# A decoder layer's self-attention: one bank of the first maxima copied aside by ScalarE, and the context products moved from POOL to VectorE

## What is computed

```python
x = x + _L0_attn_ref(_layernorm(x, axis=-1), Wq, Wk, Wv, Wo, rel_bias)

# _L0_attn_ref: H, DK = 16, 64
q, k, v = (proj(Wq), proj(Wk), proj(Wv))
scores = jnp.einsum('bhqd,bhkd->bhqk', q, k)
bias = rel_bias[_relative_position_buckets(S)]
scores = scores + bias.transpose(2, 0, 1)[None]
attn = jax.nn.softmax(scores, axis=-1)
ctx = jnp.einsum('bhqk,bhkd->bhqd', attn, v)
return ctx.transpose(0, 2, 1, 3).reshape(B, S, H * DK) @ Wo.T
```

## Time and profile before

| | us |
|---|---|
| median of three runs (lowest, highest) | 3798.07 (3797.63, 3800.9) |
| the profiled execution's own time | 3797.64 |
| its span, first to last instruction | 3795.8 |
| mean granted TensorE clock | 0.989 |

### The profile page before, as it was taken

How to read it: one execution, slowest core, us unless ns; L and a number is a source line. 1 busy time by engine, 2 the same in 40 slices (tenths; PEclk the granted TensorE clock), 3 DMA queues, 4 the chain that set the end, 5 groups by cost and what they waited for, 6 DMA issues and landing times. The chain is left out here.

```text
span 3795.8 us, 62609 instructions
## 1 busy us (share of the span) xinstructions
PE 3681.4 (97%) x21277; PEld 2195.6 (58%) x21277; DVE 2450.3 (65%) x3356; ACT 2016.1 (53%) x3452; POOL 2684.2 (71%) x1402
## 2 busy tenths in 40 slices
PE   9989999999999999999999999999979999997899
PEld 7755545555555555554555555555438888884387
DVE  3456676666666766776667776677526777774731
ACT  3336566666666665666666665666534555553232
POOL 1119999999999999999999999999963434430010
PEclk9989999999999999999999999999989999998999
DMA  7662223432234352243223333233322333335710
GB/s 222 160 145 64 70 70 82 103 76 69 70 74 106 100 139 70 70 106 83 72 68 71 99 89 72 67 72 89 92 79 76 104 97 106 105 125 197 248 37 23
DMA packets 368346, 366.60 MB, mean 97 GB/s; under 512 B 189339, under 2 KB 261531, under 8 KB 362776
## 3 DMA queue, kind: packets, MB, share of 16 engines
q1 hardware_dynamic: 299064, 336.50, 32.9%
q10 hardware_dynamic: 67168, 20.98, 2.4%
q0 software_dynamic: 1920, 6.29, 0.5%
HBM read 142.64 MB, written 89.70 MB: 61 GB/s over the span
## 5 line engine op out<-in xcount | busy, mean ns | idle before, releaser
L354 POOL TENSOR_TENSOR acc<-acc,probs 128x1024 f32<-128x1024 f32 x894 | 2131.8, 2385 | 147.0 <-ACT probs L822 35.5
L947 DVE TENSOR_REDUCE maxes<-ps 128x2 f32<-128x1024 f32 x1024 | 1251.3, 1223 | 474.2 <-PE ps L617 462.2
L825 ACT ACTIVATE probs<-ps,far_bias 128x1024 f32<-128x1024 f32 (+7 forms) x1280 | 999.0, 819 | 722.2 <-DVE near_s L964 447.1
L648 PE MATMUL ps<-probs,v_head 128*64 128x512 f32 x4096 | 993.7, 606 | 0.4 <-ACT probs L822 0.4
L636 PE MATMUL ps<-stacks 64*128 64x512 f32 x6144 | 810.9, 392 | 6.1 <-ACT probs L822 5.3
L636 PEld LDWEIGHTS ps<-stacks 64*128 64x128 f32 x6144 | 579.9, 186 | 133.3 <-ACT probs L822 12.6
L617 PE MATMUL ps<-stacks 64*128 64x512 f32 x2048 | 504.1, 490 | 17.5 <-DVE maxes L947 12.2
L617 PEld LDWEIGHTS ps<-stacks 64*128 64x128 f32 x2048 | 191.5, 184 | 565.1 <-DVE maxes L947 424.2
L648 PEld LDWEIGHTS ps<-probs,v_head 128*64 128x64 f32 x4096 | 248.6, 136 | 443.2 <-issue 441.8
L964 DVE TENSOR_TENSOR near_s<-ps,near_bias 128x384 f32<-128x384 f32 (+2 forms) x576 | 265.0, 491 | 37.2 <-PE ps L636 34.3
L970 DVE TENSOR_TENSOR c_q<-ps,c_q 64x512 fp32r<-64x512 f32 x128 | 87.5, 684 | 306.6 <-ACT c_q L781 306.6
(11 more groups left out here) (278 smaller groups left out, 4557.6 us busy)
## 6 DMA issues: line engine op xcount, KB each, us to landing
stacks<-c_q SPq DMA_DIRECT2D x128, 256.0 KB, 4.3
stacks<-c_d SPq DMA_DIRECT2D x64, 512.0 KB, 6.9
stacks<-c_k SPq DMA_DIRECT2D x32, 768.0 KB, 5.6
stacks<-c_k SPq DMA_DIRECT2D x64, 384.0 KB, 7.2
scr_v<-probs ACTq DMA_DIRECT2D x32, 512.0 KB, 4.1
v_head<-scr_v SPq DMA_DIRECT2D x32, 512.0 KB, 3.7
scr_ctx<-ctx_out SPq DMA_DIRECT2D x128, 128.0 KB, 2.3
both_ctx<-scr_ctx SPq DMA_DIRECT2D x32, 512.0 KB, 3.9
```

The lines of the kernel that those rows point to most:

```text
L354: pool.tensor_tensor(acc[:, qb, :], acc[:, qb, :], pr, ALU.add).then_inc(s["summed"], 1)
L648: mm = pe.matmul(ps[64 * half:64 * half + 64, PV, :], v_head[:, side, kt, :], probs[:, st % PT_RING, half * 512:(half + 1) * 512], start=k ...
L825: ins = act.activation(probs[:, st % PT_RING, a:z], sc[:, a:z], ACT.Exp, bias=bias)
L947: dve.tensor_reduce(maxes[:, qt:qt + HALF_GROUPS // 2 + 1:HALF_GROUPS // 2, first_chunk + pair], ps[:, bank:bank + 2, :], AX.X, ALU.max).t ...
```

## The change

ScalarE copies the second of the two banks of the first maxima into a new buffer `aside` (`set_aside`, at the start of each group that has maxima). VectorE's reduction of the first maxima covers the first bank alone, and a further reduction (`largest_aside`), behind that of the second maxima, covers `aside`. TensorE's second maxima wait for the reduction and for the copy; the copy waits for the products and for the reduction of the copy before. The context products go from POOL to VectorE, into groups 14 (`qb` = 0) and 6 (`qb` = 1 of the head before), ahead of the lowering of the queries. In the diff POOL's part comes first, then TensorE's, ScalarE's and VectorE's.

```diff
-CONTEXT_STEPS = {25: 0, 13: 1}
+CONTEXT_GROUPS = {14: 0, 6: 1}
...
+        aside = sb("aside", [P, 512])
...
-            def context(n, qb):
-
-                pool.wait_ge(s["recip_in"], 64 * n + 32 * qb + 32)
-                pool.wait_ge(s["ctx_raw"], 2 * n + qb + 1)
-                pool.tensor_tensor(ctx_out[:], ctx_out[:], sums[:], ALU.mult).then_inc(s["ctx"], 1)
...
-                    if st in CONTEXT_STEPS:
-                        of = CONTEXT_STEPS[st]
-                        if of == 0 or carry:
-                            context(n if of == 0 else n - 1, of)
...
+                if pair == 0:
+                    past(pe, s["aside"], GROUPS * m + turn)
+                elif not (isinstance(n, int) and n < 0):
+                    past(pe, s["aside"], GROUPS * m + turn + 1)
...
+            def set_aside(n, g):
+
+                late, turn = max_turn(g)
+                m = n + 1 if late else n
+                act.wait_ge(s["maxed"], GROUPS * 2 * m + 2 * turn + 1)
+                past(act, s["aside_done"], GROUPS * m + turn)
+                act.copy(aside[:], ps[:, max_bank(n, 0) + 1, :]).then_inc(s["aside"], 1)
...
                 for g in range(GROUPS):
+                    if has_max(n, g):
+                        set_aside(n, g)
                     if g == 0 and prep:
                         split_w(n + 2)
...
-                dve.tensor_reduce(maxes[:, qt:qt + HALF_GROUPS // 2 + 1:HALF_GROUPS // 2, first_chunk + pair], ps[:, bank:bank + 2, :], AX.X, ALU.max).then_inc(s["max_done"], 1)
+                if pair == 0:
+                    dve.tensor_reduce(maxes[:, qt:qt + 1, first_chunk], ps[:, bank, :].unsqueeze(1), AX.X, ALU.max).then_inc(s["max_done"], 1)
+                else:
+                    dve.tensor_reduce(maxes[:, qt:qt + HALF_GROUPS // 2 + 1:HALF_GROUPS // 2, first_chunk + 1], ps[:, bank:bank + 2, :], AX.X, ALU.max).then_inc(s["max_done"], 1)
+
+            def largest_aside(n, g):
+
+                late, turn = max_turn(g)
+                m = n + 1 if late else n
+                qt, first_chunk = max_tiles(turn)
+                dve.wait_ge(s["aside"], GROUPS * m + turn + 1)
+                dve.tensor_reduce(maxes[:, qt + HALF_GROUPS // 2:qt + HALF_GROUPS // 2 + 1, first_chunk], aside[:].unsqueeze(1), AX.X, ALU.max).then_inc(s["aside_done"], 1)
...
                 dve.wait_ge(s["max_done"], GROUPS * 2 * m + GROUPS * (half + 1))
+                dve.wait_ge(s["aside_done"], GROUPS * m + HALF_GROUPS * (half + 1))
...
+            def context(n, qb):
+
+                dve.wait_ge(s["recip_in"], 64 * n + 32 * qb + 32)
+                dve.wait_ge(s["ctx_raw"], 2 * n + qb + 1)
+                dve.tensor_tensor(ctx_out[:], ctx_out[:], sums[:], ALU.mult).then_inc(s["ctx"], 1)
...
                         largest(n, side, g, 1)
+                        largest_aside(n, g)
                     if prep and g in STEP_GROUPS:
                         step(n + 2, STEP_GROUPS[g])
                     if lowered:
                         step_lo(*lowered)
+                    if g in CONTEXT_GROUPS:
+                        qb = CONTEXT_GROUPS[g]
+                        if own if qb == 0 else carry:
+                            context(n if qb == 0 else n - 1, qb)
                     if prep and g in EVAC_GROUPS:
                         queries_low(n + 2, EVAC_GROUPS[g])
```

More of the change, by code:

```diff
@@ L253, in attention @@
             proj q_hi k_own k_hi q_lo step step_hi step_lo fill_q fill_k fill_d
-            maxed max_done neg_ready neg_stored neg_in
+            maxed max_done aside aside_done neg_ready neg_stored neg_in
             scored biased exped summed pved summ sum_out spread recip recip_stored recip_in
```

## The result

The change takes 3844.24 us (median of four runs, 3841.49 to 3847.43) beside 3797.85 for the kernel before on the same chip: a ratio of 1.0120, 95% interval 1.0107 to 1.0132. It is **slower** by 46 us, where 54 us of gain were forecast. The profiled execution took 3841.49, its span is 3839.7, and its mean granted clock 0.980 instead of 0.989. In what follows one execution, of the kernel with the context products alone, took 7044.12 us and is left out of its ratio.

The account below looks back on a forecast made before the run. TensorE (97% busy), losing 0.21 us a group to VectorE's reductions, was taken as the bound, POOL close below. 31 heads x 1.87 = 58, about 2 more, less 6: 54 us off 3798 gives 3744, range 3732 to 3758.

Parts of the forecast that it names:

- TensorE's loop: Second maxima's weight loads wait for VectorE's reduction; halving it to 512 columns gains 0.21 us a group, 1.87 us a head.
- the 1.61 of the sign: Sign of a right forecast: first to second maxima take 1.61 us in most groups instead of 1.82.
- Groups 4 and 12: Groups where ScalarE's copy follows VectorE's step and ScalarE's rounding; second maxima wait, losing 0.23 and 0.14 us.
- the rival of the full gain: Chain behind VectorE's step is not late, since VectorE and ScalarE overlap more: 91 us less 6, 3713 us; chance 0.10.
- The copies on ScalarE cost nothing elsewhere: 16 copies of 0.59, 9.4 us a head, ahead of exponentials that wait for later scores; ScalarE busy 53%; priced at nothing.
- Permission from POOL: Context products off POOL cut its work from 78.7 to 76.2 us a head; otherwise it would limit the gain to 0.8.
- the rival of a bound POOL: Each context product on VectorE keeps POOL from additions some 1.2 us: 78.6 a head, 3776 us; chance 0.13.
- Products on VectorE, covered: In groups 6 and 14 products wait for POOL's addition, up to 2.4 us, then take 0.54; VectorE's idle 2.37 covers them.
- the rival that was slower: Context product misses its turn between POOL's additions and waits another 2.5 us: 3826 to 3900, taken as 3850; chance 0.10.
- The reciprocals' arrival: VectorE waits in order for the reciprocals' broadcast, late in head 13 where SP reloads the input first: +6 us, once.
- the term of 2: 2 us added for the head behind head 13, on top of some 4 us that VectorE is held past its cover.

## Why the prediction was wrong

- **TensorE's loop (right, two groups priced too low).** Heads of 77.4 to 77.9 were forecast; those without a disturbance are 77.9 in the change and 77.8 without the loop. The reductions take 0.688 and 0.676 on average (0.69 and 0.67 forecast). A group that nothing hinders became 0.21 shorter (3.91 instead of 4.12), as forecast. (From first to second load it is 1.50 and not the 1.61 of the sign, but the load is now made ahead; the product itself begins 1.73 behind the first load, 1.72 in the forecast's working.) Groups 4 and 12 take 2.19 and 2.01 from first to second load (about 2.0 forecast), held by the copy behind step and rounding, so the rival of the full gain is out. They cost more than was priced: group 4 loses 0.39 us in the median of the heads (0.23 forecast), group 12 0.21 (0.14). With smaller differences in groups 0, 1, 5 and 9 a head gains 1.63 instead of 1.87.
- **"The copies on ScalarE cost nothing elsewhere" (wrong).** This is the step that failed. It weighed 9.4 us a head against a ScalarE that is busy for 53%, and looked at their time alone. They cost by their code: 77 instructions a pass took ScalarE's loop from three blocks to at least four, and the 13 jumps cost 86 us (3844.24 against 3757.93 without the loop), more than the whole gain. The forecast had no rival for it.
- **Permission from POOL (right).** With the products on GpSimd 78.7 a head were forecast; the copy alone shows 78.8 in most heads, and 3774 us where a gain of 0.8 a head gives 3773. That the rival of a bound POOL had nearly the same time, 3776, is chance: it was made for products on VectorE, and with these the heads are 77.8.
- **Products on VectorE, covered (right).** Alone they leave the head at 79.53. In the change they last 0.68 to 2.61 us (0.7 to 2.9 forecast), on average 1.96; 61 of the 63 end 0.55 or 0.56 behind the end of the addition that GpSimd was in when they began (0.54 forecast). None missed its turn, so the rival that was slower is out, though the sign was its own.
- **The reciprocals' arrival (right in kind, too small).** +6 was forecast, 4 in head 13 and 2 in the head behind. The products alone show 7.6 and 7.0 there (87.10 - 79.53 and 87.28 - 80.24), 14.6 us. Head 13 waits 6.4, not 4, and the term of 2 was mis-sized: the lateness of head 13 comes back, as far as the rows show, in the next head's fill of `stacks`, a wait that the forecast did not follow. In the change itself head 13 is behind a jump and its wait only 1.9. Where the products of these heads stay on GpSimd and ScalarE is written out, head 14 still loses 4.4 to 5.9 us to that fill: the heads have become shorter and the reload has not. That this is why the fill is late is not tested. How much of head 14 in the change is due to which of the two was not taken apart.

Without the jumps the change stands at 3757.93 us, and 3797 - 3758 is 39 us of the forecast 54. The 15 between are mostly the heads 13 and 14 with some 9 (15 instead of 6), and heads of 77.8 instead of 77.65 with 5.

Timeline of VectorE in the change, head 16, group 6, where the answer to the earlier trace rows can be read:

```profile
1596.72 0.67 DVE L963 TENSOR_REDUCE maxes<-aside 128x1 f32<-128x512 f32 x1
1597.32 2.44 DVE L1007 TENSOR_TENSOR ctx_out<-ctx_out,sums 128x512 f32<-128x512 f32 x1
1599.78 0.69 DVE L987 TENSOR_TENSOR c_q<-ps,c_q 64x512 fp32r<-64x512 f32 x1
1600.87 0.69 DVE L953 TENSOR_REDUCE maxes<-ps 128x1 f32<-128x512 f32 x1 [0.40 <-PE ps L612]
```

The product takes 2.44 us and the next reduction still waits for TensorE.

## What to carry to other kernels

Where an engine runs a loop, count what an edit adds to the loop's code, register instructions and waits included, and look where the loop begins; its time alone does not tell: an engine at half load can stall the others at each jump back. The sign in a profile is a first operation of a loop that waits for "issue" as many times as the loop jumps, and code transfers while the loop runs; the first remedy to try is to write that engine's loop out, which cost nothing here, and where a loop must stay, one may try to put first in it what nobody waits for soon (not tested here). And an operation that is moved to the engine of the main chain brings its worst wait along, not its usual one: look for the pass in which its input is latest, and for what the queue behind that carries on.

## What the runs showed of the hardware

- ScalarE's code was fetched 8 KB at a time, once per 128 instructions; written out, the 4800 (before) and 5800 (change) instructions ahead of its next loop ran without a stall of that kind. A loop over three such blocks jumped back in 0.24 us, one over four in 3.8 to 4.2, the same loop of 363 instructions in the one or the other by what stood ahead of it.
- After 4.8 us of idleness TensorE was granted 0.50 in all of the next 4.3 us, so that a lateness of 5.0 us cost 1.7 more in the products behind it.
- A VectorE product with both inputs in SBUF, begun within one of GpSimd's additions, ended 0.55 or 0.56 us behind that addition (61 products of the change), and the addition that followed took 2.61 to 2.67 us. GpSimd's additions take 2.382 to 2.385 us on average where GpSimd makes the context products (six kernels) and 2.402 to 2.405 where VectorE makes them all (five): 894 x 0.019 / 63 is 0.27 us for each product. So the hold is mutual, but mostly VectorE's.
